# Relative-position attention: score tiles of 32 queries x 4 heads, one stacked 96-row product, relative term on two column tiles

## The reference, cut to what matters

```python
HEAD = 8; LEFT = 64; RIGHT = 8                # 16 heads
q, k, v = proj(Wq, bq), proj(Wk, bk), proj(Wv, bv)      # (B, 16, L, 8)
attn = jnp.einsum('bhld,bhrd->bhlr', q, k) * scale
dist = jnp.clip(jnp.arange(L)[None, :] - jnp.arange(L)[:, None], -LEFT, RIGHT) + LEFT
rel = jnp.einsum('bhld,lrd->bhlr', q, dist_emb[dist]) * scale
attn = jax.nn.softmax(attn + rel, axis=-1)
out = jnp.einsum('bhlr,bhrd->bhld', attn, v)
return out.transpose(0, 2, 1, 3).reshape(B, L, H) @ Wo.T + bo
```

## Time and profile before

| | us |
|---|---|
| median of 3 runs | 1800.36 (1800.31 to 1801.09) |
| the profiled execution | 1801.48 |
| its span, first to last instruction | 1799.6 |
| first score matmul of the 16 turns | 1116.24 |
| first score matmul of the last turn | 1555.15 |
| a turn, from the second on | 29.25 to 29.44 |
| the first turn | 27.87 |

### The profile page before, as it was taken

One profiled execution on the slowest core, in us unless ns is written; L12 is line 12 of the kernel. 1 busy time (PEld: TensorE's weight loads), 2 busy tenths in 40 slices (PEclk: granted clock), 3 DMA queues, 4 the chain that ended last, 5 costly groups with the idle time before them and its releaser, 6 DMA issues.

```text
span 1799.6 us, 32035 instructions
## 1 busy us (share of the span) xinstructions
PE 1521.0 (85%) x10636; PEld 1123.0 (62%) x10636; DVE 1096.6 (61%) x2586; ACT 779.0 (43%) x1465; POOL 632.9 (35%) x558
## 2 busy tenths in 40 slices
PE   4999999999987999931559539999999999966998
PEld 2566666666654777721247326777777777755887
DVE  2666666666665454468323153777878787765554
ACT  2666666666651211210013111666666666643222
POOL 2555555555540000010431603455555546302110
PEclk7999999999996877755779856999999999987999
DMA  3331000000001000000013034000000000000000
GB/s 115 109 120 47 31 31 31 31 31 31 31 26 38 0 0 0 1 0 0 9 49 88 22 83 47 1 0 0 0 0 0 0 0 0 0 1 1 1 0 23
DMA packets 60908, 44.82 MB, mean 25 GB/s; under 512 B 8171, under 2 KB 54076, under 8 KB 60872
## 3 DMA queue, kind: packets, MB, share of 16 engines
q1 hardware_dynamic: 58824, 43.09, 8.5%
q0 software_dynamic: 2048, 1.27, 0.3%
HBM read 21.60 MB, written 10.49 MB: 18 GB/s over the span
## 4 chain that ended last, share of the span: by engine, by line
PE 31%; issue 31%; POOL 22%; DVE 10%; another core or an unknown queue 3%; ACT 1%; POOLq 1%; DVEq 1%; SPq 0%; DMA 0%; ACTq 0%
POOL arena L477 11%; PE bank L1322 5%; PE bank L991 4%; POOL a_qhigh L548 3%; POOL a_qlow L548 3%; PE bank L1305 3%; PE bank L968 3%; PE bank L981 3%; POOL a_ksplit L542 2%; PE bank L1081 2%; POOL wqkv L531 2%; PE bank L1091 1%; DVE arena L1768 1%; PE bank L1194 1%
## 5 line engine op out<-in xcount | busy, mean ns | idle before, releaser
L477 POOL TENSOR_TENSOR arena<-arena,rden 128x512 f32<-128x512 f32 x256 | 261.2, 1041 | 244.2 <-DVE rden L1406 244.2
L647 ACT ACTIVATE arena<-bank,negmax 128x512 f32<-128x512 f32 x256 | 173.8, 683 | 134.3 <-DVE negmax L1397 133.2
L1763 DVE TENSOR_REDUCE negmax<-bank 128x1 f32<-128x512 f32 x256 | 173.3, 677 | 41.4 <-PE bank L1186 40.9
L1397 DVE TENSOR_REDUCE negmax<-bank 128x1 f32<-128x512 f32 x256 | 164.3, 684 | 10.9 <-PE bank L875 7.5
L885 PE MATMUL bank<-cst,arena 128*128 128x128 f32 x1024 | 142.6, 280 | 1.4 <-DVE arena L1392 0.7
L885 PEld LDWEIGHTS bank<-cst,arena 128*128 128x128 f32 x1024 | 108.9, 141 | 51.6 <-issue 48.6
L763 ACT ACTIVATE arena<-bank 128x512 f32<-128x512 f32 x128 | 136.3, 1065 | 0.8 <-PE bank L1194 0.8
L1768 DVE COPY arena<-bank 128x512 f32<-128x512 f32 x128 | 134.9, 1054 | 0.3 <-PE bank L1194 0.3
L1186 PE MATMUL bank<-w,wqkv 128*128 (+1 forms) x512 | 133.4, 342 | 0.0
L1181 PE MATMUL bank<-a_ksplit,a_qhigh 128*128 (+1 forms) x256 | 124.3, 486 | 4.8 <-issue 3.2
L875 PE MATMUL bank<-a_qk 64*128 64x512 f32 x768 | 124.6, 429 | 0.0
(11 more groups left out here) (292 smaller groups left out, 3312.3 us busy)
## 6 DMA issues: line engine op xcount, KB each, us to landing
hst<-hT SPq DMA_DIRECT2D x32, 256.0 KB, 2.3
wst<-wqkv SPq DMA_DIRECT2D x32, 192.0 KB, 2.4
w<-in_ew SPq DMA_DIRECT2D x2, 2048.0 KB, 8.5
xs_rows<-f SPq DMA_DIRECT2D x3, 1024.0 KB, 5.0
arena<-xs_rows SPq DMA_DIRECT2D x8, 384.0 KB, 3.8
ys_rows<-wqkv SPq DMA_DIRECT2D x8, 384.0 KB, 2.9
w<-in_f1g SPq DMA_DIRECT2D x1, 1024.0 KB, 5.6
w<-in_f1u SPq DMA_DIRECT2D x1, 1024.0 KB, 8.9
```

The lines of the kernel that those rows point to most:

```text
L477: pool.tensor_tensor(a0_p[u % 4], a0_p[u % 4], rden[:, u:u + 1].broadcast_to([P, SEQ]), ALU.mult).then_inc(a0_norm, 1)
L647: act.activation(a0_p[u % 4], bank[u % 4][:, :], ACT.Exp, bias=negmax[:, u:u + 1], accum_out=den[:, u:u + 1]).then_inc(a0_exp, 1)
L1397: dve.tensor_reduce(negmax[:, u:u + 1], bank[u % 4][:, :], AX.X, ALU.max, negate=True).then_inc(a0_max, 1)
L1763: dve.tensor_reduce(negmax[:, n % 8:n % 8 + 1], bank[n % 4][:, :], AX.X, ALU.max, negate=True).then_inc(a1_max, 1)
```

## The change

A score tile becomes 32 queries x 4 heads (four tiles to a group of four heads). Only 4 x 8 = 32 rows are then needed for one factor, so three stacked pieces, (high q, low q, high q) against (high k, high k, low k), make one contraction of 96 rows: one fp32r matmul (L1228 of the new kernel) where there were two. The relative term has 16 queries as its contraction, so a tile needs two fp32 matmuls of 64 weight columns and 208 streamed columns each, on the two halves of the array's columns (L1233).

The stacks are built by DMA: SP issues 12 of 32 x 128 (`stack_q`, L476) and 12 of 32 x 512 (`stack_k`, L488) a turn. High and low q are made once for a whole sequence ahead of the turns. DVE's part is one addition of 128 x 512 a turn (`key_ends`), ACT's one copy (`high_k`), POOL's one subtraction (`low_k`) and eight spreads of 512 columns. The copies into `probTh` write runs of 128, and the values matmul reads `probTh` in runs of 16 (`a1_pT`). PE's loop goes over four sequences with four turns written out, so that the windows are constants.

```diff
+        kk = w2[:, E1:, :, :].rearrange("p e h d -> p (e h d)")[:, 4 * SEQ:5 * SEQ]
+        k_hi = over("a1_khi", [P, SEQ], "vx0", 0)
+        k_lo = over("a1_klo", [P, SEQ], "w2", E1 * 2 * D + 4 * SEQ)
+        kstack = [over("a1_kstack0", [3 * HQ * HD, HQ, SEQ], "w2", E1 * 2 * D), over("a1_kstack1", [3 * HQ * HD, HQ, SEQ], "hT", 0)]
+        q_hi = over("a1_qhi", [P, TOK], "x0buf", 0)
+        q_lo = over("a1_qlo", [P, TOK], "big_q", 0)
+        sb("a1_qroom", [P, SEQ])
+        qstack = [over("a1_qstack0", [3 * HQ * HD, HQ, P], "a1_qroom", 0), over("a1_qstack1", [3 * HQ * HD, HQ, P], "featsT", 0)]
+        qblk = over("a1_qblk", [3 * HQ * HD, 2, 2, LT, HQ, LG], "wqkv0", 0)
+        rblk = wqkv0[:, 2 * P * HG:4 * P * HG].rearrange("p (i j g h l) -> p i j g h l", i=2, j=2, h=HQ, l=LG)
...
+        def a1_to(n):
+
+            return probTh[n // 8][:, :, n % 8, :, :].rearrange("p k r l -> p k (r l)")
+
+        def a1_from(i):
+            return bank[i][:, :].rearrange("p (k c) -> p k c", k=QT)
...
+            def stack_q(it, par, b):
+
+                sp.wait_ge(a1_qhi, b + 1)
+                sp.wait_ge(a1_qlo, b + 1)
+                if not (isinstance(it, int) and it < 2):
+                    sp.wait_ge(a1_qb, it * 8 - 8)
+                for g in range(HQ):
+                    rows = slice(g * HQ * HD, (g + 1) * HQ * HD)
+                    for i, half in enumerate((q_hi, q_lo, q_hi)):
+                        sp.dma_start(qstack[par][i * HQ * HD:(i + 1) * HQ * HD, g, :].bitcast(F32), half[rows, ds(it * P, P)].bitcast(F32)).then_inc(a1_qst[par], 16)
...
+            def stack_k(it, par):
+
+                sp.wait_ge(a1_klo, it + 1)
+                if not (isinstance(it, int) and it < 2):
+                    sp.wait_ge(a1_s, it * 16 - 16)
+                if isinstance(it, int) and it == 1:
+                    sp.wait_ge(a1_pre_mm, 4 * B)
+                for g in range(HQ):
+                    rows = slice(g * HQ * HD, (g + 1) * HQ * HD)
+                    for i, half in enumerate((k_hi, k_hi, k_lo)):
+                        sp.dma_start(kstack[par][i * HQ * HD:(i + 1) * HQ * HD, g, :].bitcast(F32), half[rows, :].bitcast(F32)).then_inc(a1_kin[par], 16)
...
+            def low_k(it):
+                pool.wait_ge(a1_khi, it + 1)
+                pool.tensor_tensor(k_lo[:, :], kk, k_hi[:, :].bitcast(F32), ALU.subtract).then_inc(a1_klo, 1)
...
-                        for g in range(2):
-                            if g:
-                                pool.wait_ge(a1_split, it * 3 + 1)
-                            low = ksplit[HR:, par, g, :]
-                            pool.tensor_tensor(low, a1_kdup[g][HR:, :], low.bitcast(F32), ALU.subtract).then_inc(a1_split, 1)
...
-                    mask = bcast(bcast(halfmask, 1, LG), 1, LT)
-                    for to, q in ((qblk[hg], a1_qhi), (qlow[:, hg, :, :, :], a1_qdup)):
-                        pool.tensor_tensor(to, bcast(q[:, hg, :].rearrange("p (g l) -> p g l", l=LG), 3, HG), mask, ALU.mult).then_inc(a1_qb, 1)
+                        pool.wait_ge(a1_qst[par], rounds * STACK)
+                    for j in range(2):
+                        q = qstack[par][:, hg * 2 + j, :].bitcast(F32).rearrange("p (g l) -> p g l", l=LG)
+                        pool.tensor_tensor(qblk[:, hg, j, :, :, :], bcast(q, 2, HQ),
+                                           bcast(bcast(quadmask[0:3 * HQ * HD, :], 2, LG), 1, LT), ALU.mult).then_inc(a1_qb, 1)
+                        heads = slice((hg * 2 + j) * HQ, (hg * 2 + j + 1) * HQ)
+                        pool.tensor_tensor(rblk[:, hg, j, :, :, :], bcast(a1_q2[:, ds(it * LT, LT), heads], 3, LG),
+                                           bcast(bcast(rowmask, 1, HQ), 1, LT), ALU.mult).then_inc(a1_qb, 1)
+                    if hg == 0 and not last:
+                        low_k(it + 1)
...
+            def high_k(it, par, rounds):
+                act.wait_ge(a1_kk, it + 1)
+                if not (isinstance(it, int) and it == 0):
+                    act.wait_ge(a1_kin[1 - par], rounds * STACK)
+                act.activation(k_hi[:, :], kk, ACT.Copy).then_inc(a1_khi, 1)
...
-                    if n in (5, 8, 10) and not last:
-                        a1_high_part(it + 1, (5, 8, 10).index(n), False)
+                    if n == 4 and not last:
+                        high_k(it + 1, 1 - par, rounds)
...
-            def a1_scores(it, n, first):
-                hg, lg = n // 8, n % 8
-                if lg == 0:
-                    pe.wait_ge(a1_split, it * 3 + 3)
-                    pe.wait_ge(a1_qb, it * 6 + hg * 3 + 3)
+            def a1_scores(it, t, rounds, n, first):
+                hg, j, lg = n // 8, n // 4 % 2, n % 4 * 2
+                if n == 0:
+                    pe.wait_ge(a1_kin[t % 2], rounds * STACK)
+                if n % 4 == 0:
+                    pe.wait_ge(a1_qb, it * 8 + n // 4 * 2 + 2)
                 if not (first and n < 4):
                     pe.wait_ge(a1_exp, it * 16 + n - 3)
-                pe.matmul(bank[n % 4][:, :], qblk[hg][:, lg, :, :].rearrange("p l h -> p (l h)"),
-                          ksplit[:, ds(it % 2, 1), hg, :].rearrange("p i n -> p (i n)"), start=True, stop=False)
-                pe.matmul(bank[n % 4][:, :], qlow[:, hg, lg, :, :].rearrange("p l h -> p (l h)"),
-                          ksplit[:, ds(it % 2, 1), hg, :].rearrange("p i n -> p (i n)"), start=False, stop=False)
-                first_key = window(it % QT)
-                pe.matmul(bank[n % 4][:, ds(first_key, WIN)], rblk[hg][:, lg, :, :].rearrange("p l h -> p (l h)"),
-                          relT[:, ds((it % QT) * -P + first_key + (OFF - lg * LG), WIN)], start=False, stop=True).then_inc(a1_s, 1)
+                pe.matmul(bank[n % 4][:, :], qblk[:, hg, j, lg:lg + 2, :, :].rearrange("p g h l -> p (g h l)"), kstack[t % 2][:, n // 4, :],
+                          start=True, stop=False)
+                first_key = window(t)
+                for blk in range(2):
+                    rows = slice(blk * HQ * LG, (blk + 1) * HQ * LG)
+                    mm = pe.matmul(bank[n % 4][rows, first_key:first_key + WIN], rblk[:, hg, j, lg + blk, :, :].rearrange("p h l -> p (h l)"),
+                                   relT[:, first_key - t * P + OFF - (lg + blk) * LG:first_key - t * P + OFF - (lg + blk) * LG + WIN], start=False, stop=True)
+                mm.then_inc(a1_s, 1)
...
+        def a1_pT(hg, kt, grp, j):
+
+            return probTh[hg][:, kt, grp * LG // 4:(grp + 1) * LG // 4, :, :].rearrange("p g (b h) l -> p (g b) h l", h=HQ)[:, :, j, :]
...
-            a1_turn(0, True)
-            with pe.Fori(1, NT) as it:
-                a1_turn(it, False)
+            for t in range(QT):
+                a1_turn(t, t, t // 2 + 1, t == 0)
+            with pe.Fori(1, B) as b:
+                for t in range(QT):
+                    a1_turn(b * QT + t, t, b * (QT // 2) + t // 2 + 1, False)
...
+            def key_ends(it):
+
+                if not (isinstance(it, int) and it == 0):
+                    dve.wait_ge(a1_klo, it)
+                dve.tensor_tensor(kk, a1_k[:, ds((it // QT) * SEQ, SEQ)],
+                                  ends[:, ds(window(it % QT) * -1 + WLAST, SEQ)], ALU.add).then_inc(a1_kk, 1)
...
-                dve.tensor_copy(probTh[hg][:, :, :, lg * LG:(lg + 1) * LG].rearrange("p k h l -> p k l h"),
-                                bank[4][:, :].rearrange("p (k l h) -> p k l h", k=QT, l=LG)).then_inc(a1_tcd, 1)
+                dve.tensor_copy(a1_to(n), a1_from(4)).then_inc(a1_tcd, 1)
...
-                    if n in (2, 3, 5, 7) and not last:
-                        a1_double(it + 1, (2, 3, 5, 7).index(n), False)
+                    if n == 2 and not last:
+                        key_ends(it + 1)```

On PE, in the middle of a turn, before (`a_qhigh`, `a_qlow` are `qblk`, `qlow`; `w,wqkv` is `relT` and `rblk`; `hst`, `kT`, ... hold exponentials):

```order
L1181 MATMUL bank<-a_ksplit,a_qhigh 128x512
L1183 MATMUL bank<-a_ksplit,a_qlow 128x512
L1186 ISA
L1186 MATMUL bank<-w,wqkv 128x208
L1190 REGISTER_ALU
L1194 MATMUL bank<-cst,vtok 128x128 x4
```

112 lines of the change are left out of this document (46 added, 66 removed).

## The result

| | before | after |
|---|---|---|
| median of 4 runs each, us | 1800.72 (1800.31 to 1807.36) | 1777.28 (1774.51 to 1780.99) |
| ratio, with its 95% interval | | 0.9849 (0.9829 to 0.9868) |
| profiled execution, us | 1801.5 | 1776.34 |
| its span, us | 1799.6 | 1774.5 |
| a steady turn, us | 29.37 | 26.72 |

The change is faster by 23 us. Predicted were 1757.5 us with a range of 1738 to 1790: the sign and the range hold, the forecast promised nearly twice the gain.

What follows compares the result with a forecast made beforehand. PE's work and its waits for other engines both bound the kernel. Fifteen turns (minus 38.4), first turn (3.5), start (0.7) and end (1.3), plus 1 for jumps, made minus 42.9: median 1757.5 us, range 1738 to 1790.

Steps and rivals of the forecast that it cites:

- What bounds: In a steady turn of 29.37 us, PE's own work takes 25.4 us and its waiting 4.0 us.
- A tile: PE's work per score tile in the second layer's self-attention: 1.318 us after the change, against 1.244 before.
- edge: On PE, 0.094 us whenever the shape of the array's tiles changes, in and out of the relative term.
- no drain: Rival: tile-shape changes cost nothing inside an accumulating tile; tile about 1.02 us, total 1706 us; chance 0.08.
- serial: Rival: the relative term's four records run one after another; tile 1.67 us, turn 32.2, total 1842 us; chance 0.05.
- halfway: Rival: the relative term is three records long; tile 1.49 us, total 1795 us; chance 0.04.
- A turn: A steady turn of the second layer's self-attention: 26.8 us, including 0.2 us allowed for things not seen.
- Jumps back: PE's loop over turns: three jumps to a longer body whose code may have to be fetched, plus 1 us.
- Start: PE's wait before the first turn: POOL needs two short spreads, but the copy of v holds PE; minus 0.7 us.
- First turn: First turn from 27.87 to about 24.4 us (23.4 work, 1 waiting at tile 8), minus 3.5.
- Last turn and end: Last turn falls from 29.36 to 26.8 us; the last transposition's wait of 1.52 mostly goes, minus 1.3.
- half of the waits stay: Rival: another engine's order, not its load, makes PE late; 2 us a turn more, total 1788 us; chance 0.10.

Runs made afterwards that it cites:

- before_both: Kernel before with contiguous copies of the transposed tiles and, from the second turn, key doublings on 8 columns in place of 512; 1761.21 us, one run.
- fullrel: Changed kernel with each tile's relative term as one full-width matmul, the second block of queries getting the first's offset; 1723.61 us, one run.
- paired: Changed kernel with PE's order in pairs: two tiles' products, both relative terms, then two earlier tiles' transpositions; 1778.61 us, ratio to before 0.986.
- unrolled: Changed kernel with PE's sixteen turns written out one after the other, without its loop; 1766.4 us, ratio to before 0.9789.
- start: Changed kernel with the first turn's twelve stacked-key DMAs issued from ACT's queue instead of SP's; 1752.7 us, ratio to before 0.9836.
- paired2: Changed kernel in paired order, with ACT's copy ahead of the exponential and DVE's behind the pair's second maximum; 1734.28 us, ratio to before 0.9729.
- before_contig: Kernel before with DVE's and ACT's copies of the transposed tiles writing runs of 128 instead of strided; 1777.88 us, one run.
- before_nodouble: Kernel before with DVE's four key doublings on 8 columns in place of 512 from the second turn on; 1781.49 us, one run.
- combo2: Changed kernel with the edits of paired2, unrolled and start together; 1722.37 us, ratio to before 0.9663.

## Why the prediction was right, and where it was off

- **What bounds.** Right that both PE's work and its waits counted, and the split was right too: before_both puts PE's own work before at about 25.5 us (predicted 25.4), which leaves 3.4 us of waits and 0.4 for the jump (predicted 4.0 together). The causes named for the waits, long copies and doublings, are both shown, with 1.5 and 1.35 us; the last 0.6 stayed in before_both and is gone in the changed kernel, where PE never idles in a steady turn. DVE and ACT were expected busy for 17 to 18 and about 14 us a turn and are for 18.6 and 15.4, which costs nothing.
- **A tile.** 1.318 predicted, 1.33 measured; edge, concurrency of the two column tiles, and the late weights each as read from the earlier trace rows. fullrel and paired confirm the edges. The rivals on the tile (no drain, serial, halfway) fall. The time given for "no drain", 1706, does not follow from its turn of 23.2 us: 3.6 us less in each of 15 or 16 turns would be 1700 to 1704.
- **A turn.** 26.8 predicted, 26.71 measured. POOL and SP cost nothing in a steady turn, as said, nor do the strided streams of the values: from their first record to the next product it is 1.88 us in both kernels.
- **Where the other 18 us went.** The spans differ by 25.1, the sum said 42.9. Five terms were mis-sized. (1) Jumps back: "plus 1" for three, measured 9.8 for the two that there are, so 8.8 short. This is the step that failed: the length of the body was seen, but it was priced as a slightly longer, and the clock was not thought of. (2) Start: -0.7, measured +2.0: 2.7 short. I costed POOL's spreads and left out that 24 DMAs are issued in series ahead of the first turn behind a gather. "24 are 13 to 18 us" was there, but used for steady turns only. (3) First turn: -3.5, measured 27.87 to 27.03: 2.7 short, because it runs at clock 0.82, where the earlier trace rows had 0.92: about 9.7 us at half clock in place of 4.5, which is 2.6 us of work lost. (4) Last turn and end: -3.9, measured -1.4: 2.5 short; the wait of 1.52 became 1.07. (5) The stages behind the turns take 205.8 us where they took 203.4, with no change of code there and at a lower clock; in the unrolled run, with the same code there, they are back at the old length (rows below), so this is not the change's. Against these, the fourteen middle turns gave 1.3 us more than forecast: 8.8 + 2.7 + 2.7 + 2.5 + 2.4 - 1.3 = 17.8.

For term (5), from the layer norm behind the turns to the end, of after and of the unrolled kernel:

```profile
1568.63:1774.40 205.77, 178.47 (x1048) 153.96 (x1048) 111.22 (x316) 56.91 (x97) 28.31 (x28) 0.90 0.02 5
```

```profile
1561.03:1764.40 203.37, 176.00 (x1048) 150.94 (x1048) 111.32 (x316) 56.96 (x97) 28.35 (x28) 0.91 0.02 5
```

- **The rival "half of the waits stay"** gave 1788, 11 us above the result and nearer to it than the forecast, for another reason: in the turns no wait stayed. The upper end of the range, 1790, was there for this rival alone. That the measured time lies in the range is therefore in part luck: the 18 us that were missing came from terms for which the range had no room of its own.

The net of it: PE's new order of work gained nothing in a turn (26.71 us, where the old matmuls took 26.53 in before_both with a jump and 0.6 us of waits in each, and about 25.5 by themselves). The 0.23 us saved on the low product went into the edges. The gain came from the waits, and what the edges cost was had back by pairing (25.51 us a turn).

## What to carry to other kernels

When a change writes out more turns in a loop body, price its jump back apart: here two jumps cost 2.9 and 2.7 us, and half clock for 3.4 and 6.5 us behind them, 9.8 of a gain of some 33 us. Where an engine's tile shape has to change inside a tile, group the same shapes of several tiles, and move the copies of the following engines with them, or they give the gain away. Where two engines' work stands ahead of a wait, take each away alone and both together before one is called the cause (here 1.5, 1.35 and 2.85 us), and look at the work ahead of the first turn as closely as at the turn.

## What was not expected of the hardware

- At a jump back of PE's loop the weight loads stand for 0.47 us and the turn loses 0.4 with a body of one turn (about 265 records of matmuls); with one of four turns (over 1,000) they stand for 2.7 to 3.9 us. Straight code of sixteen turns has no such stops, though packets come on the instruction queue all along it.
- A stop of 2.7 to 3.9 us at a jump is followed by 3.4 to 7 us at the lower granted level (1.2 GHz). That is so at 12 of the 14 such jumps in the seven kernels that have them; at one of start's and one of paired2's the clock stays at 1.00 behind a stop just as long. In the kernels without long stops (before, before_contig, before_nodouble, before_both, unrolled, combo2) it stays at 1.00 from the second turn to the last. So no drop came inside the turns without a stop, but the stop doesn't decide it alone; what else does is open.
- The first DMA issue behind the element-wise gather took 6.2 to 6.8 us on the queue that issued the gather, while issues on another queue took 0.62 at the same time.
- Two matmuls on two column tiles (64 weights columns each, 208 columns streamed) cost 0.31 us a tile more than one of full width, when they stand between full-width work.
